# Attention maxima split and transposed by quad, with PSUM handed out by single banks

## The chip, the cores and the metric

One core of one Trainium2 chip runs the whole kernel. The metric is the device time of one execution in microseconds; it is quoted as the median of several runs. Five engines work from queues of their own, each strictly in the order in which it was written: TensorE (PE; its weight loads are shown as PEld), VectorE (DVE), ScalarE (ACT), GpSimd (POOL) and SyncE (SP), which here issues nearly all DMAs.

## The reference

A decoder block on x of 8 batches x 256 tokens x 128 features, in float32, with a context of 64 tokens for each batch:

```python
x = layernorm(x + self_attn(x))                # 16 heads of 8 dims, rotary q and k, no mask
x = layernorm(x + cross_attn(x, ctx, mask))    # 16 heads, 64 keys, mask * -1e9, a dense layer behind it
x = layernorm(x + relu(x @ W1 + b1) @ W2 + b2) # 128 -> 512 -> 128

scores = einsum('bhqd,bhkd->bhqk', q, k) / sqrt(8)
probs = softmax(scores, axis=-1)               # needs the maximum over the keys of each query and head
ctx = einsum('bhqk,bhkd->bhqd', probs, v)
```

## The kernel before

The 16 heads of the self-attention are four *quads* g of four heads each. For each batch b, quad g and half t of the queries, `max_scores(b, g, t)` (L603) writes the scores with queries on the partitions (use `Mgt`, 128 x 1024) to PSUM, and VectorE's `reduce(b, g, t)` (L1535) takes the maximum over the keys of four heads. When all eight reductions of a batch are done, `split_max(b)` (L1541, L1545) turns the maxima of all quads into a high and a low part in two instructions. `max_transposes(b)` (L613) transposes them on TensorE (use `mT`), and ScalarE's `maxT(b)` (L1193) copies them, 32 rows by 1024 columns, below the query rows of `q_rows`. Only then come the second scores: `exp_scores(b, g, half)` (L625, uses `Egh`, 128 x 1024) has keys on the partitions and subtracts the maxima in the same product, because `k_diag` has rows that pick the head (`diag_heads`, `head_of_row`). `exp(b, g, half)` (L1202) on ScalarE makes the probabilities, and `pv(b, half)` (L642) multiplies them with v.

The cross-attention has the same form with fewer keys: `maxx_scores` (`Xm`, L699), `reduce(b, "x", t)` (L1532), `split_maxx`, `maxx_transposes` (`mxT`), `maxxT` (L1234), `expx_scores` (`Y`, L718), `expx` (L1246) and `pvx` (L731). Its mask is put into PSUM ahead of each product by `preset_mask`: 22 times on ScalarE (L1163) and 10 times on VectorE (L1665). Behind it are a dense layer (L759), the feed-forward layers `ffn_up` (L779) and `ffn_down` (L790), and three layer norms. ScalarE's other copies out of PSUM are `pv_copy` (L1209) and `pvx_copy` (L1256).

The q and k of a batch go through DRAM to be laid out: GpSimd rotates them (`rope_cosine`, `rope_sine`, `rope_sum`, `qk_high`, `qk_low`), SP writes images to `z_self` and reads them back with `load_q(b)` (L369, one DMA) and `load_k(b)` (L377, four DMAs). There are two copies of `q_rows` and `k_diag`, so both loads of batch b wait, in `rows_free`, until all eight `E` products of batch b - 2 are made. The first two batches are rotated on VectorE instead (`first_products`, `first_rotated`, `first_low`).

PSUM is five *spaces*: `s0`, `s1` and `s2` of two banks each, `b0` and `b1` of one bank. A table `USES` lists for each space all its uses in order, written out by a search; `TURN` gives the place of a use, and each engine waits for the reader of the use before (`earlier`). A small use in `s0` to `s2` holds both banks. The order of all calls on each of the five engines is a list written out by hand or by a search as well: hundreds of calls on TensorE, VectorE and ScalarE, about a hundred on GpSimd and on SP.

## Time and profile before

| what | us |
|---|---|
| median of 3 runs | 221.43 (220.69 to 223.17) |
| the profiled execution, its own time | 223.62 |
| its span, from the first to the last instruction | 221.8 |
| busy: PE, PEld, DVE, ACT, POOL | 202.8, 152.1, 173.4, 166.1, 93.6 |
| mean granted TensorE clock | 0.988 of full speed |

The profile is of one execution. Matmul ends are modelled and matmuls are pipelined, so that "PE busy" counts some time in which a product only drains. Lines of a timeline merge instructions of one group: start, time from the first start to the last end, engine, line, what it writes and reads, how many, and in brackets the idle time of the engine before it with what ended it.

### The profile page before, as it was taken

Reading aid. Unit: us, or ns where it says so; the run is one execution under the profiler, and the core shown is the slowest. Engines: PE = TensorE matmul, PEld = TensorE weight load, DVE = VectorE, ACT = ScalarE, POOL = GpSimd, SP = SyncE. Lnnn points to the kernel's source line nnn. Section 1 sums busy time; section 2 is a strip of 40 time slices with the busy share of each in tenths; the row PEclk is TensorE's granted clock in tenths of the full one; section 3 lists DMA queues with packets and bytes.
Section 4 is the critical chain, followed back from the end, with each engine's and each line's share of the span. In section 5 each row is a group of like instructions: output and inputs, shape, how many; then the busy total and the mean of one; then the engine's idle time right before and its main releaser. Section 6 shows DMA issues by size and latency. Waiting matters only on the chain.

```text
span 221.8 us, 5032 instructions
## 1 busy us (share of the span) xinstructions
PE 202.8 (91%) x1632; PEld 152.1 (69%) x1632; DVE 173.4 (78%) x346; ACT 166.1 (75%) x248; POOL 93.6 (42%) x130
## 2 busy tenths in 40 slices
PE   7777989999898979999989998999999999999991
PEld 5555657666476546767657667776987868977991
DVE  6585998448967987848988977898788879885764
ACT  2256567778188678969998898999899997896360
POOL 9304997048085776903103600710261343221533
PEclk9996999999999999999999999999999999999998
DMA  6967639414558861743650361140230234100011
GB/s 195 400 194 219 188 86 334 115 54 159 164 173 269 206 184 36 236 145 103 192 176 5 113 192 55 56 143 1 75 92 0 99 98 112 65 3 24 23 53 47
DMA packets 21354, 28.20 MB, mean 127 GB/s; under 512 B 5424, under 2 KB 16688, under 8 KB 21328
## 3 DMA queue, kind: packets, MB, share of 16 engines
q1 hardware_dynamic: 20696, 27.08, 39.8%
q10 hardware_dynamic: 632, 0.79, 1.3%
q8 instruction: 14, 0.23, 0.4%
q14 instruction: 12, 0.10, 0.2%
HBM read 14.76 MB, written 11.27 MB: 117 GB/s over the span
## 4 chain that ended last, share of the span: by engine, by line
PE 66%; issue 6%; DVE 6%; ACT 5%; DMA 2%; SPq 1%; POOLq 0%; POOL 0%; ACTq 0%; DVEq 0%
PE bank L642 12%; PE scores L625 11%; PE scores L603 10%; ACT probs L1202 4%; PE bank L779 4%; PE scores L699 3%; PE bank L790 3%; PE scores L718 3%; PE scores L779 3%; PE bank L731 3%; PE scores L790 2%; DVE max_parts L1535 2%; DMA k_diag<-z_self 2%; PE bank L671 1%; PE bank L759 1%
## 5 line engine op out<-in xcount | busy, mean ns | idle before, releaser
L1535 DVE TENSOR_REDUCE max_parts<-scores 128x4 f32<-128x1024 f32 x64 | 75.7, 1217 | 18.3 <-PE scores L603 18.1
L1202 ACT ACTIVATE probs<-scores 128x1024 f32<-128x1024 f32 x64 | 63.3, 1025 | 8.0 <-PE scores L625 7.4
L603 PE MATMUL scores<-k_diag,q_rows 96*128 96x512 f32 x128 | 44.0, 434 | 6.4 <-issue 4.2
L625 PE MATMUL scores<-q_rows,k_diag 128*128 128x256 f32 x256 | 43.0, 297 | 2.3 <-ACT probs L1202 1.3
L625 PEld LDWEIGHTS scores<-q_rows,k_diag 128*128 128x128 f32 x256 | 34.5, 189 | 12.3 <-issue 7.4
L603 PEld LDWEIGHTS scores<-k_diag,q_rows 96*128 96x128 f32 x128 | 20.7, 193 | 15.5 <-issue 13.7
L1973 POOL TENSOR_TENSOR rstd<-mean_var,minus_half 128x2 f32<-128x2 f32 x23 | 15.8, 696 | 36.1 <-DVE mean_var L1569 36.0
L642 PE MATMUL bank<-probs,v_ones 128*32 128x256 f32 x512 | 30.9, 382 | 0.1
L1163 ACT COPY scores<-cross_sb 128x1024 f32<-128x1024 f32 x22 | 22.4, 1028 | 2.5 <-DVE maxx_parts L1532 2.0
L642 PEld LDWEIGHTS bank<-probs,v_ones 128*32 128x32 f32 x512 | 15.6, 109 | 11.7 <-issue 3.3
L1532 DVE TENSOR_REDUCE maxx_parts<-scores 128x16 f32<-128x1024 f32 x16 | 19.1, 1216 | 3.9 <-PE scores L699 3.9
L1980 POOL TENSOR_TENSOR sum<-att,xT_sb 128x256 f32<-128x256 f32 x8 | 5.9, 738 | 28.5 <-DVE att L1615 28.4
L1999 POOL TENSOR_TENSOR qx_parts<-qx_parts 128x256 fp32r<-128x256 f32 x8 | 5.8, 728 | 27.2 <-ACT qx_parts L1226 27.2
L1246 ACT ACTIVATE probsx<-scores 128x1024 f32<-128x1024 f32 x16 | 16.2, 1028 | 0.8 <-PE scores L718 0.7
L2025 POOL TENSOR_TENSOR qk_sin<-qk_swapped,rope_sb 128x256 f32<-128x256 f32 x12 | 8.5, 728 | 18.2 <-DMA qk_swapped<-qk 18.2
L1576 DVE TENSOR_SCALAR x<-sum,mean_var,rstd 128x128 f32<-128x128 f32 x32 | 11.8, 409 | 2.5 <-POOL rstd L1973 2.5
L1665 DVE COPY scores<-cross_sb 128x1024 f32<-128x1024 f32 x10 | 12.2, 1218 | 0.7 <-ACT probsx L1246 0.5
L718 PE MATMUL scores<-qx_slots,kx_diag 128*128 128x256 f32 x64 | 11.0, 296 | 0.7 <-ACT qx_slots L1234 0.7
L699 PE MATMUL scores<-kx_diag,qx_slots 96*128 96x256 f32 x64 | 11.2, 300 | 0.4 <-issue 0.4
L1209 ACT COPY ctxvT<-bank 128x256 f32<-128x256 f32 x16 | 5.8, 372 | 7.0 <-PE bank L642 7.0
L718 PEld LDWEIGHTS scores<-qx_slots,kx_diag 128*128 128x128 f32 x64 | 8.8, 189 | 2.5 <-ACT qx_slots L1234 1.3
L1565 DVE BATCH_NORM_STATS2 stats<-sum 128x6 f32<-128x128 f32 x42 | 10.0, 279 | 0.2
(174 smaller groups left out, 358.4 us busy)
## 6 DMA issues: line engine op xcount, KB each, us to landing
z_self<-qk_parts SPq DMA_DIRECT2D x21, 256.0 KB, 2.7
q_rows<-z_self SPq DMA_DIRECT2D x8, 384.0 KB, 4.1
qx_slots<-z_qx SPq DMA_DIRECT2D x8, 384.0 KB, 3.6
k_diag<-z_self SPq DMA_DIRECT2D x30, 96.0 KB
z_qx<-qx_parts SPq DMA_DIRECT2D x8, 256.0 KB, 2.2
qk_swapped<-qk SPq DMA_DIRECT2D x12, 128.0 KB, 2.8
xT_sb<-x SPq DMA_DIRECT2D x4, 256.0 KB, 3.3
z_qx<-qx_parts SPq DMA_DIRECT2D x8, 128.0 KB, 1.7
```

Of the source, the lines that this page charges most:

```text
L603: mm = pe.matmul(score(use, b)[:, h * S:(h + 2) * S], qr_r[0:NROWS, b % 2, g, t * P:(t + 1) * P], kd_r[0:NROWS, b % 2, h:h + 2, g, :], sta ...
L625: mm = pe.matmul(score(use, b)[:, (2 * j + kt) * S:(2 * j + kt + 1) * S], kd_r[:, b % 2, 2 * half + j, g, kt * P:(kt + 1) * P], qr_r[:, b ...
L642: mm = pe.matmul(misc(use, b)[STRIP * h:STRIP * (h + 1), 0:S], v_ones[:, b % 2, kt, HQ * g + h, cell], probs[:, g, h, kt, :], start=(g % 2 ...
L699: mm = pe.matmul(score(use, b)[:, g * 256:(g + 1) * 256], qxs_r[0:NROWS, b % 2, g, t * P:(t + 1) * P], kxd_r[0:NROWS, b % 2, g, :, :], sta ...
L718: mm = pe.matmul(score(use, b)[:, (p % 4) * S:(p % 4 + 1) * S], kxd_r[:, b % 2, p // 2, 2 * (p % 2):2 * (p % 2) + 2, :], qxs_r[:, b % 2, p ...
L779: mm = pe.matmul(misc(use, b)[:, j * S:(j + 1) * S], const("w1")[:, c * P:(c + 1) * P], x2T_of[turn(b)], start=True, stop=True)
L1163: ins = nc.scalar.copy(score(use, b).rearrange("p (n c) -> p n c", c=SC if use[0] == "X" else S), mask)
L1202: ins = nc.scalar.activation(probs[:, g, 2 * half:2 * half + 2, :, :], score(use, b), ACT.Exp, scale=KSCALE)
L1246: ins = nc.scalar.activation(probsx[:, 4 * half:4 * half + 4, :], score(use, b), ACT.Exp)
L1532: ins = nc.vector.tensor_reduce(quads(maxx_parts, b, 1)[:, t * QUADS:(t + 1) * QUADS, 0:HQ], score(use, b).rearrange("p (g h k) -> p g h k ...
L1535: ins = nc.vector.tensor_reduce(max_parts[:, b % 2, 1, t, g * MROWS:g * MROWS + HQ], score(use, b).rearrange("p (h k) -> p h k", h=HQ), AX ...
L1973: nc.gpsimd.tensor_tensor(rstd[:, k, :], mean_var[:, k, :, 1], minus_half[:], ALU.pow).then_inc(rstd_done[n], 1)
```

## The change

- Each quad is split alone: `split_max(b, g)` takes 8 maxima of each partition (4 heads by 2 halves), `max_transposes(b, g)` transposes both halves in one step (a 128 x 64 block, the halves 32 rows apart), and `maxT(b, g)` copies 8 rows by 128 columns twice. `exp_scores(b, g, half)` waits for its own quad's copy alone. There are 32 such steps in place of 8.
- The cross-attention's maxima stay in one step for each batch, but their block is 32 wide for each quad, and `maxxT` copies 8 rows by 256 columns four times in place of 32 rows by 1024 once.
- The other rows of `q_rows` and `qx_slots` must be zero: GpSimd clears both at the start (`clear_rows`, `clear_qx`), and `load_q`, `load_qx`, `maxT` and `maxxT` wait for that. VectorE clears `max_parts` and `maxx_parts` in `clear_parts`, which now stands ahead of its `clear_diag`.
- PSUM is eight single banks. Scores take a pair (0-1, 2-3, 4-5 or 6-7) and small uses one bank; `earlier` is now a list of waits, one for each different use before.
- All orders and the table of banks are new. Presets of the mask are 17 on ScalarE and 15 on VectorE. On VectorE `kx_split` and `place_vx(0)` come behind batch 0's reductions, on SP `load_cross` and `load_ctxT` behind batch 0's q and k.

```diff
 USES = {
-    "s0":
-        "qp.0 v.4 kp.1 vxa.0 M01.0 M21.0 M31.0 M00.1 M30.1 E10.0 E21.0 E11.0 E31.0 mT.1 E00.1 M01.2 M31.2 E20.1 "
...
+    0:
+        "qkp.5 M20.0 M01.0 M10.0 mT0.0 E31.0 M20.1 E20.0 E10.0 E01.1 E00.1 M20.2 E31.1 E10.2 mT0.2 M20.3 M21.3 "
...
+    1:
+        "M20.0 M01.0 M10.0 mT1.0 E31.0 M20.1 E20.0 E10.0 PV0.0 E01.1 E00.1 M20.2 E31.1 E10.2 M20.3 M21.3 E20.2 "
...
-        scores = psum("scores", [P, 3, 1024])
-        bank = psum("bank", [P, 2, 512])
+        banks = psum("banks", [P, BANKS * BANK])
...
         def earlier(use, b):
 
-            space, before = TURN[use, b]
-            return read[space], before
+            return [taken(*previous) for previous in dict.fromkeys(TURN[use, b][2])]
...
-            def max_transposes(b):
-                pe.wait_ge(max_split, b + 1)
+            def max_transposes(b, g):
+                pe.wait_ge(max_split[g], b + 1)
                 pe.wait_ge(wv_in, 16)
-                if TURN["mT", b][1]:
-                    pe.wait_ge(*earlier("mT", b))
-                for t in range(QT):
-                    mm = pe.transpose(misc("mT", b)[0:XROWS, t * P:(t + 1) * P], max_parts[:, b % 2, 0, t, :], ident)
-                written_by(mm, "mT", b)
+                for previous in earlier(f"mT{g}", b):
+                    pe.wait_ge(*previous)
+                mm = pe.transpose(misc(f"mT{g}", b)[0:QT * STRIP, 0:P], max_parts[:, b % 2, g, :, :], ident)
+                written_by(mm, f"mT{g}", b)
 
             def exp_scores(b, g, half):
                 use = f"E{g}{half}"
-                pe.wait_ge(*taken("mT", b))
+                pe.wait_ge(*taken(f"mT{g}", b))
...
-            def maxT(b):
-                act.wait_ge(*made("mT", b))
+            def maxT(b, g):
+                act.wait_ge(*made(f"mT{g}", b))
+                act.wait_ge(rows_zeroed, 1)
                 if b > 1:
-                    for products in all_made(EXPONENTS, b - 2):
-                        act.wait_ge(*products)
-                ins = nc.scalar.copy(q_rows[max_rows, b % 2, :, :].bitcast(F32R),
-                                     misc("mT", b)[0:XROWS, 0:S].rearrange("p (o c) -> p o c", o=1).to_broadcast([XROWS, QUADS, S]))
-                read_by(ins, "mT", b)
+                    act.wait_ge(*made(f"E{g}0", b - 2))
+                    act.wait_ge(*made(f"E{g}1", b - 2))
+                for t in range(QT):
+                    ins = nc.scalar.copy(q_rows[max_rows, b % 2, g, t * P:(t + 1) * P].bitcast(F32R),
+                                         misc(f"mT{g}", b)[t * STRIP:t * STRIP + MROWS, 0:P])
+                read_by(ins, f"mT{g}", b)
...
-            def split_max(b):
-                for maxima in all_taken(MAXIMA, b):
-                    dve.wait_ge(*maxima)
-                if b > 1:
-                    dve.wait_ge(*made("mT", b - 2))
-                split(max_parts, b, max_hi_done, max_split)
+            def split_max(b, g):
+                dve.wait_ge(*taken(f"M{g}0", b))
+                dve.wait_ge(*taken(f"M{g}1", b))
+                exact = max_parts[:, b % 2, g, :, MROWS:MROWS + HQ].rearrange("p t (h o) -> p t h o", o=1)
+                nc.vector.tensor_reduce(max_parts[:, b % 2, g, :, 0:HQ].bitcast(F32R), exact, AX.X, ALU.max, negate=True
+                                        ).then_inc(max_hi_done[g], 1)
+                dve.wait_ge(max_hi_done[g], b + 1)
+                both = max_parts[:, b % 2, g, :, 0:2 * MROWS].rearrange("p t (a h) -> p t h a", a=2)[:, :, 0:HQ, :]
+                nc.vector.tensor_reduce(max_parts[:, b % 2, g, :, HQ:MROWS], both, AX.X, ALU.add, negate=True
+                                        ).then_inc(max_split[g], 1)
...
             clear_y()
+            clear_parts()
             clear_diag()
             first_products(0, 1)
             first_rotated(0, 1)
+            first_low(0, 1)
             first_products(0, 0)
-            first_low(0, 1)
```

## Rows read from the trace of the kernel before

**Rows 1.** The page, part 1: busy time, share, instructions of each engine

```profile
PE 202.8 (91%) x1632; PEld 152.1 (69%) x1632; DVE 173.4 (78%) x346; ACT 166.1 (75%) x248; POOL 93.6 (42%) x130
```

**Rows 2.** Windows of three stages: length, busy us of each engine (instructions), granted clock

```profile
32.00:80.00 48.00, 43.81 (x376) 29.83 (x374) 35.37 (x52) 33.01 (x42) 27.45 (x41) 1.00 0.61 178
80.00:137.00 57.00, 53.98 (x468) 38.35 (x469) 46.91 (x77) 51.75 (x68) 19.86 (x29) 1.00 0.44 134
137.00:214.00 77.00, 76.18 (x662) 62.35 (x661) 63.42 (x165) 65.55 (x109) 25.09 (x36) 1.00 0.19 58
```

**Rows 3.** Timeline of VectorE and ScalarE between batches, 41 to 63 us

```profile
46.72 0.36 DVE L1613 RECIPROCAL recip<-bank 128x32 f32<-128x32 f32 x1 [5.00 <-PE bank L654]
...
57.27 0.37 ACT L1209 COPY ctxvT<-bank 128x256 f32<-128x256 f32 x1 [1.59 <-PE bank L642]
60.28 0.37 ACT L1209 COPY ctxvT<-bank 128x256 f32<-128x256 f32 x1 [2.63 <-PE bank L642]
...
62.42 1.00 ACT L1193 CAST q_rows<-bank 32x1024 fp32r<-32x1024 f32 x1
```

**Rows 4.** Timeline of SP's loads of batches 2 and 3, and TensorE's first maxima products

```profile
41.64 3.03 SPq L377 DMA_DIRECT2D k_diag<-z_self  x4
...
54.57 2.98 SPq L377 DMA_DIRECT2D k_diag<-z_self  x4
...
47.37 1.22 PE L603 MATMUL scores<-k_diag,q_rows 96*128 96x512 f32 x4 [0.21 <-issue]
...
61.07 0.70 PE L603 MATMUL scores<-k_diag,q_rows 96*128 96x512 f32 x2 [0.86 <-issue]
```

**Rows 5.** Timeline of the start, from the first products to the first exponential

```profile
5.87 0.48 DVE L1587 SCALAR_TENSOR_TENSOR qk_cos<-scores,wk_sb,rope_sb 128x256 f32<-128x256 f32 x1 [0.47 <-DMA rope_sb<-rope]
...
19.17 2.36 DVE L1535 TENSOR_REDUCE max_parts<-scores 128x4 f32<-128x1024 f32 x2 [1.90 <-PE scores L603]
...
19.70 1.40 POOL L2025 TENSOR_TENSOR qk_sin<-qk_swapped,rope_sb 128x256 f32<-128x256 f32 x2 [11.95 <-DMA qk_swapped<-qk]
...
22.28 6.88 DVE L1535 TENSOR_REDUCE max_parts<-scores 128x4 f32<-128x1024 f32 x6 [0.76 <-PE scores L603]
...
29.25 0.19 DVE L1541 TENSOR_REDUCE max_parts<-max_parts 128x32 fp32r<-128x32 f32 x1
...
30.27 1.00 ACT L1193 CAST q_rows<-scores 32x1024 fp32r<-32x1024 f32 x1 [0.78 <-PE scores L613]
...
32.19 1.02 ACT L1202 ACTIVATE probs<-scores 128x1024 f32<-128x1024 f32 x1
```

**Rows 6.** Groups by line and form: shapes, count, busy us, mean ns of one

```profile
L1541 DVE TENSOR_REDUCE max_parts<-max_parts 128x32 fp32r<-128x32 f32 x8 | 1.5, 186 | 0.6 <-DVE max_parts L1535 0.2
L1545 DVE TENSOR_REDUCE max_parts<-max_parts 128x32 f32<-128x64 f32 x8 | 1.8, 221 | 0.3
L1193 ACT CAST q_rows<-scores 32x1024 fp32r<-32x1024 f32 x5 | 5.0, 1000 | 2.2 <-PE scores L613 2.2
L1209 ACT COPY ctxvT<-bank 128x256 f32<-128x256 f32 x16 | 5.8, 372 | 7.0 <-PE bank L642 7.0
L1256 ACT COPY attvT<-bank 128x512 f32<-128x512 f32 x7 | 4.1, 589 | 0.3 <-PE bank L731 0.2
L1163 ACT COPY scores<-cross_sb 128x1024 f32<-128x1024 f32 x22 | 22.4, 1028 | 2.5 <-DVE maxx_parts L1532 2.0
L1665 DVE COPY scores<-cross_sb 128x1024 f32<-128x1024 f32 x10 | 12.2, 1218 | 0.7 <-ACT probsx L1246 0.5
L1631 DVE TENSOR_SCALAR attvT<-bank,cross_sb 128x512 f32<-128x512 f32 x1 | 0.8, 750 | 0.0
```

**Rows 7.** The chain that ended last: start, us, what

```profile
30.01 0.22 PE scores L613 x2
...
67.35 0.70 PE scores L603 x2
...
145.46 0.47 PE scores L603 x2
```

More of the change, by code:

```diff
@@ L120, in turns @@
     at = {}
-    for space, uses in USES.items():
-        for before, use in enumerate(uses.split()):
+    for bank in range(BANKS):
+        signals, previous = 0, None
+        for use in USES[bank].split():
             name, b = use.split(".")
-            at[name, int(b)] = space, before
+            key = name, int(b)
+            if key not in at:
+                at[key] = bank, signals, []
+                signals += 1
+            if previous:
+                at[key][2].append(previous)
+            previous = key
     return at
@@ L561, in warm_up @@
                 for _ in range(3):
-                    pe.matmul(bank[:, 1, 0:S], y[:, 0, :], y[:].rearrange("p t d -> p (t d)"), start=True, stop=True)
+                    pe.matmul(banks[:, 7 * BANK:7 * BANK + S], y[:, 0, :], y[:].rearrange("p t d -> p (t d)"), start=True, stop=True)
             def first_proj(b, j):
@@ L1156, in preset_mask @@
                 act.wait_ge(mask_ready, 1)
-                act.wait_ge(*earlier(use, b))
+                for previous in earlier(use, b):
+                    act.wait_ge(*previous)
                 if use[0] == "X":
@@ new lines, in _ @@
+            expx(3, 1)
+            exp(7, 3, 0)
+            exp(7, 2, 1)
+            maxxT(4)
+            exp(7, 2, 0)
+            expx(4, 1)
+            pv_copy(7, 0)
+            x2T_copy(1)
+            pvx_copy(3)
+            pv_copy(7, 1)
+            expx(4, 0)
+            x1T_copy(6)
+            preset_mask("Xm1", 5)
+            qx_copy(6)
+            att2T_copy(3)
+            preset_mask("Y1", 5)
+            relu(1, 0)
+            pvx_copy(4)
+            maxxT(5)
+            relu(1, 1)
@@ L1773, in _ @@
+            reduce(0, 1, 1)
+            split_max(0, 3)
+            reduce(0, 1, 0)
+            split_max(0, 0)
+            split_max(0, 1)
+            split_max(0, 2)
+            kx_split()
+            place_vx(1)
+            reduce(1, 0, 1)
+            reduce(1, 1, 0)
+            reduce(1, 2, 0)
+            place_vx(0)
+            reduce(1, 1, 1)
+            reduce(1, 2, 1)
+            split_max(1, 2)
+            scale_mask()
+            split_max(1, 1)
             reduce(1, 0, 0)
+            split_max(1, 0)
@@ L1854, in _ @@
[L1854 to L1868 removed]
+            split_max(6, 0)
+            reduce(6, 3, 1)
+            reduce(6, 2, 0)
```

1445 lines of the change are left out of this document (737 added, 708 removed), and 58 rows, old and new, of the table USES.

## The prediction, made before the changed kernel was run

> **What bounds the kernel now.** I read the page's busy shares first. TensorE is the fullest engine at 202.8 us of a span of 221.8, with VectorE at 78% and ScalarE at 75% [rows 1]. A mean over the span hides three different stages, so I then cut the span into windows. From 32 to 80 us no engine is full: VectorE is busy 35.4 of 48 us, ScalarE 33.0, and TensorE's weight loads, which stand for how many products went through, fill 29.8 us, or 62% [rows 2]. From 80 to 137 us ScalarE is busy 51.8 of 57 us (91%), VectorE 82%, weight loads 67%. From 137 to 214 us weight loads fill 81% and matmuls 76.2 of 77 us: there TensorE is the bound, because the feed-forward layers need almost nothing of the others.
>
> What takes the time of the first stage is seen between the batches. After the split of batch 1's maxima VectorE sits idle for 5.00 us. ScalarE sits idle for 1.59 and then 2.63 us after the last exponential of batch 1, and gets batch 2's maxima only at 62.42 us [rows 3]. A batch is a chain of phases: eight reductions, one split, one transpose, one copy, eight exponentials. One of the two readers of PSUM is often without work while the other has its phase. The second link is the load of q and k: it waits for all E products of two batches earlier, SP issues k's DMAs from 41.64 to 44.67 us, and the first maxima product of batch 2 starts at 47.37; for batch 3 they start at 54.57 and the product comes at 61.07 [rows 4]. So a load costs some 6 us from k's first DMA, and what releases it is the end of the phase of exponentials.
>
> The chain that ended last shows the third loss: a pair of maxima products takes 0.47 us when the PSUM space is free and 0.70 us when TensorE must stop for it or behind it [rows 7].
>
> **The start.** The first exponential starts at 32.19 us, behind eight reductions of batch 0 (19.17 to 29.16), a split at 29.25, and a copy of 1.00 us from 30.27 [rows 5]. After the change the first split follows the seventh reduction, which saves one reduction of 1.15 us (6.88 us for six). The copy is two of 128 columns. ScalarE took 372 ns for 256 columns and 589 ns for 512 [rows 6], 0.85 ns a column, so 128 columns are 0.26 us each and the copy 0.53 in place of 1.00. Only one weight block is transposed in place of two: 0.11 us less. The smaller split saves under 0.1. Sum: 1.15 + 0.47 + 0.11 + 0.1 = 1.8 us, and I take -1.8. Against it stand VectorE's two new clearings of 512 elements, at most half a preset copy of 1.22 us each and so 1.2 us, of which 0.47 is hidden by the wait for the rotary table [rows 5], and `first_low(0, 1)`, which now stands with its wait for ScalarE ahead of q's products. For it, `load_cross` and `load_ctxT` no longer compete with the first loads, and k's DMAs, the last to be issued before, go ahead of q. I take these at nothing between them, with bounds of -1 and +1.5 us. GpSimd's two further clearings lie in the 11.95 us for which it is idle ahead of 19.70 us [rows 5]; without the cover `load_q(0)` waits, and the whole start with it.
>
> **What is added.** VectorE: a split of 32 elements takes 186 ns and one of 64 elements 221 ns [rows 6], so 1.1 ns an element over a fixed 151. With 8 and 16 elements it is 160 + 169 = 0.33 us for a quad, 10.5 us for 32 quads, less the 3.3 of before: +7.2 us. Five presets of the mask come over at 1.22 us: +6.1. `kx_split` and `place_vx(0)` (0.75 us for the first instruction [rows 6], some 2 us in all as an estimate from it) move out of an idle time into the run of reductions: +2. The sum is about +15 us, of which 0.9 (four quads less the old split of 0.41) falls to batch 0. ScalarE: 64 copies at 0.263 us less eight at 1.00 are +8.8. `maxxT` with 32 copies at 0.372 in place of eight at 1.00 is +3.9. Five presets at 1.03 leave: -5.1. The sum is +7.6 us. TensorE: 32 transposes in place of 16 at 0.11 (0.22 for two [rows 7]) are +1.8 us, and each is a point at which it can stop: between 0 and 32 times the 0.23 us by which 0.70 exceeds 0.47, so 0 to 7.4 us. I take 1.6 for the last stage's share of all this. The further waits on the lists of banks have no row of their own; between nothing and 0.05 us for each score product (an estimate, a tenth of a 0.47 us pair), I take nothing, since the engines' queues run ahead of satisfied waits.
>
> The Trainium skill ("VectorE: DVE Perf Modes", section on the TRN2 errata) speaks against this change: a fixed latency is paid for each instruction, and tiles should have 512 elements or more. The trace agrees as to size, since its fixed part of 151 ns [rows 6] is near the page's some 150 cycles; by the rule alone the change is a loss of the whole sum above.
>
> **What is gained.** In 32 to 214 us VectorE is busy 145.7 of 182 us and ScalarE 150.3 [rows 2]. After the change VectorE has about 160 us to do there and ScalarE about 158. With the start 1.8 us earlier, an unchanged time needs VectorE's idle time to fall from 36 to 24 us. Can it? Between batches the 5.00 us and the 4.2 us of rows 3 go for the most part: the exponentials of the first quad run beside the reductions of the last. The last E product of a batch then comes 2 to 3 us earlier against its first reduction, and the load of the batch after next with it. A fourth pair of banks also lets a product be ready while both readers are at work. For 32 to 80 us, where all engines are under 75% but for modelled matmul time, I take -2.8 us, net of the added work: more than one bubble of 5 us is removed, and 3.5 us of splits and copies are added. For 80 to 137 us ScalarE at 91% and VectorE at 82% take up what the finer steps free: 0, with bounds of -2 and +4. For 137 to 214 us TensorE is full: +1.6.
>
> The Trainium skill ("Perfetto Trace Analysis", Identifying the Most-Contended Engine) holds that matmul busy time misleads, and that the share of weight loads tells the headroom. By its rule the last stage at 81% would have up to a fifth to give, some 14 us as an estimate. The 0.47 us pair in that stage [rows 7] is without a stop, so the trace does not show such a headroom.
>
> The sum: -1.8 - 2.8 + 0 + 1.6 = -3.0 us. The profiled execution took 223.62 us, 1.8 more than its span, and stands 2.2 above the median of 221.43; I take the difference from the median: 218.4.
>
> **The rivals.**
>
> *A fuller flow.* The barrier costs at every junction, not only at the first two, and the fourth pair of banks removes most 0.70 us stops. Then 80 to 137 us gives 2 to 3 us as well and the first stage 4 or 5: 214.5. For it speaks that the loop from E products through a load to the maxima products is shortened for each batch. Against it, VectorE would have to be over 92% busy for 180 us.
>
> *VectorE becomes the bound (slower).* Its added 15 us lie in the stages in which it feeds everything: splits sit in its queue ahead of reductions, and each reduction holds two banks. It decides from the point at which less than 12 us of its idle time is recovered. If just the bubble of 5.0 us and some 3 us more go, the time is +15 - 8 - 1.8 = +5 us: 226.5. For it: no stage of the kernel before has all three engines at nearly 90%. Against it: the idle time is mostly waiting for TensorE, which the additions do not load. The skill's rule on small tiles, above, would lead here.
>
> *A draw.* The idle time is only exchanged for small instructions, and the earlier start is given back before the last stage: 221.4.
>
> *It does not do what it says.* If the order lists let each quad's transposes wait in TensorE's queue behind products of other batches, exponentials start no earlier within a batch. That has the price of the second rival, and I count it there.
>
> **How the numbers follow.** Chances: forecast 0.42, fuller flow 0.13, draw 0.22, VectorE the bound 0.23. About 1% (2.2 us) is what a measurement of this kernel can tell from no change. Four fifths of the forecast's share lie under 219.2 us, as does all of the fuller flow; so faster 0.47. The draw and the rest of the forecast, and a small part of the third case, make same 0.29; slower 0.24. The bounds of the start (-1, +1.5), of the middle stage (-2, +4) and of TensorE's stops reach from 213 to 225, which leaves a tenth out on either side.
>
> **What would show it.** The first exponential at about 30.4 us in place of 32.19. VectorE busy near 188 us and ScalarE near 174. No idle time of over 3 us on VectorE between 35 and 65 us. The last exponential of the self-attention 4 to 5 us earlier, and a last stage that is 1 to 2 us longer. The prediction is wrong if the first maxima product comes after 19 us, if VectorE's idle time ends mostly on TensorE still, or if ScalarE's small copies take much over 0.26 us.

## The result

The changed kernel takes 225.77 us (224.91 to 226.56, 4 executions), the kernel before beside it 221.06 us (220.33 to 223.17, 4 executions): a ratio of 1.019, 95% interval 1.015 to 1.023. It is slower by 4.2 us by the ratio and 4.7 by the medians. The forecast was 218.4 us and a gain. Its profiled execution took 225.86 us, 1.86 more than its span of 224.0 us. Executions over 1.5% above the fastest of their kernel are left out of every ratio in this text.

Busy shares first, as in [rows 1]:

```profile
PE 205.4 (92%) x1648; PEld 155.3 (69%) x1648; DVE 185.9 (83%) x401; ACT 173.5 (77%) x323; POOL 97.7 (44%) x132
```

Then the three stages, as in [rows 2], the last one up to the end of the span, and below them that last stage of the kernel before, also up to its end:

```profile
32.00:80.00 48.00, 45.73 (x394) 32.26 (x393) 42.24 (x80) 37.52 (x65) 30.78 (x44) 1.00 0.60 185
80.00:137.00 57.00, 54.43 (x470) 38.46 (x468) 49.56 (x92) 51.62 (x91) 18.75 (x27) 1.00 0.43 128
137.00:224.00 87.00, 79.80 (x688) 64.89 (x686) 72.02 (x193) 69.00 (x135) 27.17 (x39) 0.99 0.19 57
...
137.00:221.80 84.80, 79.30 (x688) 65.28 (x686) 67.04 (x180) 65.97 (x109) 27.02 (x39) 0.99 0.19 59
```

VectorE has 12.5 us more to do and ScalarE 7.4. VectorE's idle time fell from 48.4 us (221.8 - 173.4) to 38.1, so 10.3 us were recovered where the prediction put the break-even at 12. In the first stage more products were done than before (394 against 376), so the flow there is fuller, as intended. It is given back later: from 137 us to its end the kernel before takes 84.8 us (221.8 - 137) and the changed one 87.0, with 688 products in both. The two profiled executions are 2.2 us apart in span, since that of the kernel before stands above its median; so the stages show about half of the loss of 4.7 us.

The costs of the small instructions, by form:

```profile
L1227 ACT CAST q_rows<-banks 8x128 fp32r<-8x128 f32 x64 | 16.3, 255 | 6.6 <-PE banks L620 5.6
...
L1270 ACT CAST qx_slots<-banks 8x256 fp32r<-8x256 f32 x32 | 11.6, 363 | 0.9 <-PE banks L715 0.3
...
L1600 DVE TENSOR_REDUCE max_parts<-max_parts 128x8 f32<-128x16 f32 x32 | 5.5, 171 | 1.1
...
L1596 DVE TENSOR_REDUCE max_parts<-max_parts 128x8 fp32r<-128x8 f32 x32 | 4.9, 152 | 0.6
```

These are the estimates of the prediction (0.263, 0.372, 0.169 and 0.160 us) within 6%. The sizes of the added work were right; what they do to the time was not.

The start, beside [rows 5]:

```profile
8.64 0.48 DVE L1640 SCALAR_TENSOR_TENSOR qk_cos<-banks,wq_sb,rope_sb 128x256 f32<-128x256 f32 x1
...
18.99 2.07 PE L611 MATMUL banks<-k_diag,q_rows 96*128 96x512 f32 x4 [3.84 <-DMA q_rows<-z_self]
...
23.70 5.75 DVE L1588 TENSOR_REDUCE max_parts<-banks 128x4 f32<-128x1024 f32 x5 [1.10 <-PE banks L611]
...
29.37 0.15 DVE L1596 TENSOR_REDUCE max_parts<-max_parts 128x8 fp32r<-128x8 f32 x1
...
29.90 1.31 ACT L1202 CAST kx_diag<-wv_sb 8x256 fp32r<-8x256 f32 x4
31.11 2.15 ACT L1227 CAST q_rows<-banks 8x128 fp32r<-8x128 f32 x8
...
33.82 1.04 ACT L1236 ACTIVATE probs<-banks 128x1024 f32<-128x1024 f32 x1
```

The first exponential comes at 33.82 us, not at 30.4, and 1.6 us after that of before (32.19). The first maxima product is 0.86 us late (18.99 against 18.13). These two distances belong to this execution: in another one of the same kernel (`after_again`, below) the first maxima product comes at 18.19 and the first exponential at 31.31. After seven reductions the first split stands at 29.37, later than the split after eight was before (29.25). A transposed quad must then wait for ScalarE, which is at `kx_heads` until 31.21, and all eight copies are made in one run, so the quads are not taken one by one.

From the wait ahead of those first scores up to 24 us TensorE ran at the lower of its two clock levels (1.2 GHz in place of 2.4). Windows of 2 us; the last but two column is the granted clock:

```profile
16.00:18.00 2.00, 0.00 (x0) 0.00 (x0) 0.92 (x2) 0.73 (x2) 2.00 (x2) 0.79 0.88 230
18.00:20.00 2.00, 1.01 (x2) 0.83 (x3) 0.00 (x0) 0.00 (x0) 1.76 (x1) 0.50 1.04 310
...
22.00:24.00 2.00, 1.96 (x7) 1.27 (x7) 0.90 (x2) 1.50 (x4) 1.80 (x4) 0.51 0.99 381
```

The fall comes in the 3.84 us in which TensorE waits for the q rows. The profiled execution of the kernel before has such a fall too, a shorter one, behind a wait of 2.29 us:

```profile
18.00:20.00 2.00, 1.87 (x5) 1.50 (x6) 0.83 (x1) 1.93 (x4) 0.29 (x1) 0.59 0.93 300
20.00:22.00 2.00, 2.00 (x6) 1.58 (x6) 1.52 (x2) 0.27 (x1) 2.00 (x3) 0.56 0.38 96
```

The chain that ended last also has two pieces that [rows 7] did not have: SP's four loads of kx for batch 2 (line 427, 113.44 to 116.96 us) and batch 3 (131.87 to 135.1), ahead of the load of qx:

```profile
131.87 3.22 SPq L427 DMA_DIRECT2D kx_diag<-z_kx  x4
...
135.26 0.38 SPq L445 DMA_DIRECT2D qx_slots<-z_qx  x1
```

So five explanations stood side by side: (A) the small instructions themselves, (B) the order, with the cross-attention late, (C) the late start, (D) the kx loads, and, from the spread of the executions, (G) TensorE's clock. A sixth question (E) was what single banks are worth without the quads, and a seventh (F, H) whether quads pay in an order that fits them.

### The profile page after: what moved, and what is told of

It is laid out like the page before. It is cut to its first block, busy times and chain, and to the rows that moved or that the text cites. A ratio compares the mean times of both kernels' runs of the same rounds, so it can differ in the third digit from the quotient of the medians.

```text
span 224.0 us, 5412 instructions
## 1 busy us (share of the span) xinstructions
PE 205.4 (92%) x1648; PEld 155.3 (69%) x1648; DVE 185.9 (83%) x401; ACT 173.5 (77%) x323; POOL 97.7 (44%) x132
## 4 chain that ended last, share of the span: by engine, by line
PE 63%; DVE 13%; issue 8%; DMA 5%; ACT 5%; SPq 4%; POOL 1%; POOLq 0%; DVEq 0%; ACTq 0%
PE banks L649 13%; PE banks L632 10%; PE banks L611 9%; DVE max_parts L1588 7%; PE banks L797 6%; PE banks L786 5%; PE banks L725 4%; SPq L427 3%; PE banks L706 3%; PE banks L738 3%; DMA q_rows<-z_self 3%; PE banks L766 2%; DMA qx_slots<-z_qx 2%; PE banks L748 2%; PE banks L620 1%
## 5 line engine op out<-in xcount | busy, mean ns | idle before, releaser
L1588 DVE TENSOR_REDUCE max_parts<-banks 128x4 f32<-128x1024 f32 x64 | 75.9, 1218 | 15.3 <-PE banks L611 15.3
L1236 ACT ACTIVATE probs<-banks 128x1024 f32<-128x1024 f32 x64 | 63.4, 1025 | 4.0 <-PE banks L632 2.9
L611 PE MATMUL banks<-k_diag,q_rows 96*128 96x512 f32 x128 | 44.2, 434 | 5.7 <-DMA q_rows<-z_self 3.8
L632 PE MATMUL banks<-q_rows,k_diag 128*128 128x256 f32 x256 | 42.9, 296 | 1.6 <-DVE vx_ones L1697 0.5
L632 PEld LDWEIGHTS banks<-q_rows,k_diag 128*128 128x128 f32 x256 | 34.7, 189 | 11.2 <-issue 8.4
L649 PE MATMUL banks<-probs,v_ones 128*32 128x256 f32 x512 | 30.9, 382 | 0.8 <-DVE max_parts L1588 0.3
L611 PEld LDWEIGHTS banks<-k_diag,q_rows 96*128 96x128 f32 x128 | 20.7, 197 | 12.1 <-issue 6.5
L1588 DVE TENSOR_REDUCE maxx_parts<-banks 128x16 f32<-128x1024 f32 x16 | 19.3, 1216 | 2.6 <-PE banks L706 2.5
L1719 DVE COPY banks<-cross_sb 128x1024 f32<-128x1024 f32 x15 | 18.1, 1219 | 1.0 <-ACT probs L1236 0.6
L1195 ACT COPY banks<-cross_sb 128x1024 f32<-128x1024 f32 x17 | 17.5, 1032 | 0.6
```

The costliest lines, as they stand in the source:

```text
L611: mm = pe.matmul(score(use, b)[:, h * S:(h + 2) * S], qr_r[0:NROWS, b % 2, g, t * P:(t + 1) * P], kd_r[0:NROWS, b % 2, h:h + 2, g, :], sta ...
L632: mm = pe.matmul(score(use, b)[:, (2 * j + kt) * S:(2 * j + kt + 1) * S], kd_r[:, b % 2, 2 * half + j, g, kt * P:(kt + 1) * P], qr_r[:, b ...
L649: mm = pe.matmul(misc(use, b)[STRIP * h:STRIP * (h + 1), 0:S], v_ones[:, b % 2, kt, HQ * g + h, cell], probs[:, g, h, kt, :], start=(g % 2 ...
L1195: ins = nc.scalar.copy(score(use, b).rearrange("p (n c) -> p n c", c=SC if use[0] == "X" else S), mask)
L1236: ins = nc.scalar.activation(probs[:, g, 2 * half:2 * half + 2, :, :], score(use, b), ACT.Exp, scale=KSCALE)
L1588: ins = nc.vector.tensor_reduce(out, score(use, b).rearrange("p (h k) -> p h k", k=SC if g == "x" else S), AX.X, ALU.max)
```

## The experiments

All ratios are to the kernel before in the same job, whose median there was 222 to 223 us. All re-ordered kernels below move whole calls on an engine's list, change the table of banks, and may give a mask preset to the other of its two engines; no other instruction is altered by it.

**The small instructions at the old places.** `quads_coarse` is the kernel before, with

```
 def split_max(b):
-    split(...)                      # all quads at once, 2 instructions
+    for g in range(QUADS):
+        split_quad(b, g)            # 8 instructions
 def maxT(b):
-    nc.scalar.copy(q_rows[max_rows, ...], misc("mT", b)[...])
+    for g in range(QUADS):
+        for t in range(QT):
+            ins = nc.scalar.copy(q_rows[max_rows, b % 2, g, t * P:(t + 1) * P].bitcast(F32R), ...)
```

and the changed kernel's four copies for `maxxT` and its clearings. The order of the calls and the uses of PSUM are those of the kernel before.

> The kernel before with its own order on all engines and its own PSUM spaces; only the maxima are split quad by quad (8 small splits instead of 2), transposed by 4 instructions of 64 rows instead of 2 of 128, and copied by 8 copies of 8 rows instead of one of 32 rows, all at the places of the old ones, and the exponents still wait for all of them. It carries the added small work of the change and none of what that work buys. Added in each batch between the last reduction and the first exponent: 6 splits more (about 1.0 us), 2 transposes more (0.4 us), and 7 copies of 0.25 us (1.8 us) less what the one large copy took (1.0 us): some 2 us, 8 times. Theory A (the small instructions cost the time): this stretch is a barrier in every batch, so 230 to 238 us. Theory B (order: the added work is hidden behind other engines' work and the loss of the changed kernel comes from its order): 221 to 225 us here.

It took 235.03 us: ratio 1.055 (1.048 to 1.062). The chain that ended last shows the barrier; its columns are start, length, what:

```profile
30.72 0.25 ACT q_rows L1220
...
32.57 0.26 ACT q_rows L1220
32.84 0.14 issue
32.97 0.73 PE banks L648 x4
```

`q_rows` copies have 6% of that chain. From the end of a batch's last reduction to the end of its last copy the eight batches together take 46.1 us here and 31.0 in the kernel before, 1.9 us more for each. So the small instructions, those of the cross-attention with them, cost 12 us when they stand on the barrier. The changed kernel is slower by 4 us alone; but it has the single banks and another order as well, so this run does not say how much of the 12 us it hides behind other work.

**Half of the small instructions out of the changed kernel.** `after_light` leaves out the second split instruction and the copy for the last 128 queries, so the low part of the maxima is zero, and for half of the queries the rows of `q_rows` stay as `clear_rows` left them: no maximum is subtracted there.

> The changed kernel with half of the added small work of the self-attention left out: each quad's split keeps its first instruction and leaves out the second, so that the low part of the maxima stays zero (32 VectorE instructions of 171 ns, 5.5 us), and each quad's maxima are copied to the rows of q for the first 128 queries alone (32 ScalarE copies of 255 ns, 8.2 us). TensorE's work and all orders stay. Theory A (the small instructions cost the time): 13.6 us of work on the two engines less, half of it on the path between maxima and exponents, so the time falls by 4 to 7 us, to 219 to 222 us. Theory B (order): both engines idle 17 and 23 per cent of the span, and the last 40 us are bound by TensorE's own order, so it falls by at most 2 us, to 224 us or more.

224.9 us, ratio 1.008 (1.004 to 1.013), against 1.019 for the changed kernel: about 1.1%, 2.4 us, for 13.6 us of work. That is below what A asked for, and B's limit of 2 us lies within the noise of this difference (some 0.6%, from the two intervals). The small instructions have a part that is clear of noise; whether the order has one is not decided here.

**The start repaired.** `after_start`:

```
-            clear_parts()
             clear_diag()
             first_products(0, 1)
             first_rotated(0, 1)
-            first_low(0, 1)
             first_products(0, 0)
+            first_low(0, 1)
             first_rotated(0, 0)
             first_low(0, 0)
+            clear_parts()
```

> The changed kernel; on VectorE the clearing of the maxima tiles (0.96 us) goes from ahead of the first products to behind them, and the low part of q's first image goes back behind the second pair of products. Everything else is as in the changed kernel. Theory C (the late start, first exponent at 33.8 instead of 32.2 us, reaches the end): the first scores come about 1.1 us earlier and the time falls by 1 to 1.6 us, to 224.3 to 224.8 us. Theories A and B (the start is absorbed, since the self-attention of batches 3 to 6 runs 4 to 7 us ahead anyway): within 0.5 us of the changed kernel, 225.3 to 226 us.

Ratio 1.016 (1.010 to 1.023). The ratio is 0.3% less than 1.019, well inside the interval. Its first exponential is at 32.88 us, 0.94 earlier than in the changed kernel's execution above, but the edit can't be given that: `after_loads`, the next run, has the unchanged start and its first exponential at 32.77. So C is not decided by this run: the start's order is worth some 0.6 us at most by the ratios, and nothing that the trace shows.

**The kx loads behind qx.** `after_loads`:

```
-            load_kx(2)
             qx_image_high(2)
             ...
             load_qx(2)
+            load_kx(2)
```

and the same for batch 3.

> The changed kernel; on SyncE the loads of kx for batches 2 and 3 (four DMAs each) stand behind the load of qx of the same batch instead of ahead of it. Theory D (these loads stand on the path: the chain has SyncE at 113.4 to 117.0 and 131.9 to 135.1 us, with qx's load behind them): each of the two stretches gives back about 3 us to the cross-attention of batches 2 and 3, and if that is what ends last, the time falls by 1.5 to 3 us, to 223 to 224.5 us. Theories A and B: the cross-attention of these batches waits for TensorE's order anyway, so within 0.6 us of the changed kernel.

Ratio 1.016 (1.010 to 1.023). The trace shows the load of qx for batch 3 freed, and its product not. SP's queue, then TensorE:

```profile
130.91 0.32 SPq L445 DMA_DIRECT2D qx_slots<-z_qx  x1
...
137.72 0.72 PE L706 MATMUL banks<-kx_diag,qx_slots 96*128 96x256 f32 x4 [0.22 <-ACT banks L1195]
```

The load is issued at 130.91 in place of 135.26 us, 4.35 earlier; the maxima product of that batch starts at 137.72 in place of 138.90, and the whole of these 1.18 us was already there at 114 us (another product of the line starts at 113.69 in place of 114.93). It stood on TensorE's list behind other work. D falls, by the trace and not by the ratio: a piece of the chain that ended last is not a piece that costs.

**The changed kernel again**, as a standard:

> The changed kernel itself once more, as the standard for the runs beside it: 1.015 to 1.023 times the kernel before.

Ratio 1.0185 (1.008 to 1.029). Its executions gave G: (clock, us) were (1.000, 224.24), (0.988, 227.28), (0.976, 228.02) and (0.965, 230.15), while the seven of before beside it had 0.996 to 1.000. A line through the four has 1.6 us for each 0.01 of the mean clock. That is a hint and no more: it rests on the two longest, which are not in the ratio, and in the four executions of the result above the fastest (224.91 us) has 0.984 and the slowest (226.56) 0.991.

The profiled execution of this run, at 224.24 us, is the same kernel as that of the result, at 225.86, and has no fall of the clock. It shows what the start is without one:

```profile
16.00:18.00 2.00, 0.00 (x0) 0.00 (x0) 1.48 (x2) 0.92 (x3) 2.00 (x3) 1.00 1.00 278
18.00:20.00 2.00, 1.81 (x12) 1.65 (x12) 1.05 (x1) 0.14 (x1) 2.00 (x1) 1.00 1.06 251
...
18.19 1.19 PE L611 MATMUL banks<-k_diag,q_rows 96*128 96x512 f32 x4 [2.32 <-DMA q_rows<-z_self]
...
31.31 1.04 ACT L1236 ACTIVATE probs<-banks 128x1024 f32<-128x1024 f32 x1
```

TensorE waited 2.32 us instead of 3.84, the q rows having landed earlier, and kept its clock; the first exponential comes 2.51 us earlier than at 33.82, and the span is 1.9 us shorter (222.1 against 224.0). How much of this is the clock and how much the earlier landing, two executions do not tell.

**Re-ordered from the first call on.** Three kernels, the order of before and of the changed kernel searched by moving one call at a time with durations from the profiles.

> The kernel before with its own instructions (one split and one 32-row copy of the maxima per batch) and its own five PSUM spaces; only the order of the calls on every engine, the space of each use and the engine of the mask presets are searched anew: one call moved at a time, kept when the end comes earlier with the durations read from the profile. Theory B (what the order is, is worth several us either way, and the changed kernel has an order that delays the cross-attention): a better order exists for the old instructions too: 212 to 218 us on the scale where before is 221.4. Theory A (only the work counts; the old order was as good as its work allows): 219.5 to 222.5 us.

> As the re-ordered kernel before, from the same starting order and with the same search, but PSUM is kept by eight single banks, so that a transposed tile or a projection takes one bank where it took a space of two; the maxima are still split, transposed and copied batch by batch. If single banks are worth something by themselves (theory E), it is 2 to 5 us faster than the re-ordered kernel before: 209 to 215 us on the scale where before is 221.4. If they are worth nothing, within 1 us of it.

> The changed kernel with its quad-wise maxima and its single banks, its start repaired as in the run of the start, and orders, banks and places of the presets searched anew in the same way and with the same effort. Theory B: the changed kernel's loss lay in its order, so this is well below it, 213 to 218 us, and below the kernel before. Theory A, in the form that the added small work costs the same in any order: it stays 3 to 6 us above the kernel with single banks and batch-wise maxima that was searched with the same effort. Theory F (quad-wise maxima pay once the order fits them): it is as fast as that kernel or faster.

Ratios 1.070 (1.062 to 1.078), 1.070 (1.062 to 1.078) and 1.092 (1.085 to 1.098): all far slower than either kernel. They say nothing of A, B or E, since two things went wrong. The first is likely the larger, because one execution of `before_order` kept a mean clock of 0.999 and still took 235.64 us. They had been costed with a score product group at 0.48 us and no delay between a signal and TensorE's next product; measured when nothing kept it waiting the group takes 0.55, and the delay is 0.145. Second, TensorE lost its clock in the start. Windows of `before_banks_order`:

```profile
20.00:30.00 10.00, 7.38 (x24) 4.94 (x24) 9.03 (x8) 5.82 (x13) 9.68 (x12) 0.83 0.66 201
30.00:40.00 10.00, 8.64 (x26) 6.15 (x27) 8.58 (x10) 4.82 (x6) 6.59 (x11) 0.53 0.58 162
```

In these three kernels some mask presets of the cross-attention were placed behind a narrow tile in their banks (3, 11 and 11 of the 32), and the three kernels give wrong results; that the masks of those score tiles are lost is the likely reason, see the last section.

**Re-ordered from 45 us on**, with the start as it is and each preset behind a full score tile:

> The kernel before with its own instructions and its five PSUM spaces; the order of the first 45 us is left as it is on every engine, and the rest is re-ordered by moving one call at a time with the durations read from the profiles so far; each mask preset stays behind a full score tile in its space. The three kernels that were re-ordered from the first call on lost TensorE's clock (mean grant 0.95 to 0.97, with stretches near 0.5 between 20 and 50 us), which this leaves out. Theory B (order is worth several us): 216 to 219 us on the scale where before is 221.4. Theory A (before's order is as good as its work and its five spaces allow): 220 to 223 us.

> The same search and the same frozen start of the kernel before, with PSUM kept by eight single banks; the maxima stay batch by batch. Theory E (single banks by themselves are worth something, because a projection or a transposed tile no longer blocks two banks): 2 to 5 us faster than the one with five spaces, 213 to 217 us. If they are worth nothing, within 1 us of it.

> The changed kernel, quad-wise maxima and single banks, with its start repaired and frozen up to 45 us, and the rest re-ordered by the same search with the same effort. Theory B (the changed kernel's loss is its order): 213 to 218 us, below both kernels. Theory A (the small instructions cost the time in any order): 3 us or more above the re-ordered kernel with single banks and batch-wise maxima, 217 to 222 us. Theory F (quad-wise maxima pay for themselves once the order fits): within 1 us of that kernel or below it, although its start is 1 us later.

Ratios 1.022 (1.016 to 1.029), 1.010 (1.004 to 1.015) and 1.020 (1.011 to 1.028). Every theory's number was missed: none is faster than before. Only the order among the three is of use, since single banks helped by 1.2%. The durations were still the wrong ones.

**TensorE kept at work in the start's wait.** `after_busy` and `before_busy`:

```
+            def keep_busy(n):
+                for previous in earlier("M30", 0):
+                    pe.wait_ge(*previous)
+                for _ in range(n):
+                    pe.matmul(misc("M30", 0)[:, 0:S], y[:, 0, :], y[:].rearrange("p t d -> p (t d)"), start=True, stop=True)
...
             qk_proj(7)
+            keep_busy(8)
             max_scores(0, 3, 0)
```

> The changed kernel with 8 products of the zeroed y tile (256 columns each, written to the bank of the first score tile ahead of it, read by nobody) between the last early projection and the first score product of batch 0, where TensorE waited 3.84 us for the q rows. Nothing else changes. Theory G (part of the loss is TensorE's clock: in the executions so far the mean grant was 0.983 for the changed kernel and 0.992 to 0.998 for the one before, the fall comes right behind this wait, and over the executions of one kernel 0.01 of clock went with 1.6 us of time): the clock goes to 0.995 or more and the time falls by 1 to 2.5 us, to a ratio of 1.008 to 1.014. If the clock has no part, the ratio stays at 1.018.

> The kernel before with 5 such products in the same place, where TensorE waited 2.29 us. Theory G: its clock was already 0.992 to 0.998 in the mean, so it gains 0 to 1 us, and its executions scatter less. If the clock has no part: no change, or up to 0.4 us slower where a product is still running when the rows land.

`after_busy` has 1.011 (1.006 to 1.015) against 1.0185 and 1.019 without; `before_busy` 1.002 (0.999 to 1.006). In the trace of `after_busy`:

```profile
18.00:20.00 2.00, 2.00 (x14) 1.77 (x13) 1.00 (x1) 0.10 (x1) 1.66 (x1) 1.00 1.02 280
...
22.00:24.00 2.00, 2.00 (x13) 1.67 (x12) 2.00 (x3) 2.00 (x4) 1.87 (x3) 1.00 0.86 338
```

The clock stays at 1.00 through the wait, VectorE is at work in all of 20 to 24 us, the reductions run without a stop, and the first exponential is at 31.35 us, 2.47 earlier. So the products keep the clock up in the start, and the fall is part of what made it late. What that is worth at the end stays open. By the ratios it is 0.8%, some 1.8 us, but the two kernels were measured beside different executions of the kernel before, and the interval of `after_busy` only touches that of the result (1.015) and lies inside that of `after_again` (1.008 to 1.029). `after_again`'s execution at clock 1.00 without the products took 224.24 us, and the one profiled here 225.39, with the first exponential at the same time to 0.04 us. In two of the six executions the mean clock was still 0.98 and 0.99. For the kernel before the products are worth nothing that can be measured; its first exponential in `before_busy` is at 31.18:

```profile
31.18 1.02 ACT L1208 ACTIVATE probs<-scores 128x1024 f32<-128x1024 f32 x1
```

**The measured costs in the search.** The same re-ordering, now with 0.55 us for a group of score products and the 0.145 us, and with `keep_busy` in the start:

> Single banks with batch-wise maxima, the same 5 products, the first 45 us in before's order, and the rest re-ordered once more, now with the cost that each call had in the traces when nothing kept it waiting (a group of score products 0.55 us, not 0.48) and 0.145 us from a signal to TensorE's next product. Theory E (single banks are worth 2 to 4 us once the order uses them): 215 to 219 us on the scale where before is 221.4. If the earlier re-ordered kernels failed because before's order can't be bettered: 221 us or more.

> The changed kernel's own calls (quad-wise maxima, single banks, its own first 45 us with 8 such products), the rest re-ordered in the same way and with the same effort as the run beside it. Theory B (the loss is the order of the changed kernel): 217 to 221 us on the scale where before is 221.4, so well below the changed kernel. Theory A (the small instructions cost the time in any order): 3 us or more above the kernel beside it. Theory F (quad-wise maxima pay once the order fits): as fast as that kernel, although its first scores come 1 us later.

> The kernel before with its own five PSUM spaces and batch-wise maxima, 5 products in the wait of the start, its first 45 us as they are, and the rest re-ordered with the measured costs as in the run with single banks that came to 217.1 us (ratio 0.972). Theory E (the single banks carry that gain): 2 to 5 us slower than that run, 219 to 222 us. If the order alone carries it: within 1 us of it, 216 to 218 us.

> Quad-wise maxima on single banks again, but started from the order of the 217.1 us run and with before's first 25 us on every engine (GpSimd's two clearings ahead of it), and re-ordered from there with the same effort. It tells whether the 6.6 us between batch-wise and quad-wise maxima come from the changed kernel's own start and order, which the run of 223.7 us still had in its first 45 us. If they do (theory H): 217 to 219 us. If the small instructions cost the time in any order (theory A: VectorE 10 us more than the batch-wise kernel, ScalarE 8 us more, 16 more points at which TensorE can stop): 3 us or more above the batch-wise run, 220 to 224 us.

> The run of 217.1 us (batch-wise maxima, single banks, 5 products in the start's wait), re-ordered a little further, now from 25 us on. If what limits it is still the order: 1 to 2 us faster, 214.5 to 216.5 us on the scale where before is 221.4. If TensorE's own work, busy 202 of 214.5 us, leaves no more: within 1 us of 217.1.

| kernel | maxima | PSUM | ratio to before | 95% interval |
|---|---|---|---|---|
| before_busy (before's order) | batch | five spaces | 1.002 | 0.999 to 1.006 |
| before_order3 | batch | five spaces | 0.990 | 0.985 to 0.995 |
| before_banks3 | batch | single banks | 0.972 | 0.968 to 0.975 |
| before_banks4 | batch | single banks | 0.973 | 0.968 to 0.977 |
| after_order3 (changed kernel's start) | quad | single banks | 1.002 | 0.998 to 1.007 |
| quads_order (before's start) | quad | single banks | 1.000 | 0.997 to 1.003 |
| after_busy (changed kernel's order) | quad | single banks | 1.011 | 1.006 to 1.015 |

The lines are read in pairs that differ in one feature of the kernel; each line has an order of its own from the same search, so how well the search did is part of every distance. A new order alone takes 1.2% off the kernel before. Single banks take a further 1.7 to 1.8%, so E holds. Quads in place of batches put 2.7 to 3.1% on, whichever start they have: A holds, F and H fall. The changed kernel's own order is 0.8% worse than what the same search found for the same calls. That is in the direction of B, but at 221.9 us on the scale where before is 221.4 it misses B's forecast of 217 to 221, and the two intervals just touch; B holds in a small part at most. The part of B that blamed the late cross-attention falls: its first exponentials start at 79.10 us in `quads_order` and at 91.21 in `after_order3`, and the two take the same time.

Summed up, `keep_busy` +0.2, a searched order -1.2, single banks -1.8, quads +3.1 and the changed kernel's order +0.8 give the 1.1% of `after_busy`. These are the steps between the lines of the table, so the sum is no check of them. The last 0.8%, from 1.011 to the 1.019 of the changed kernel, is what the start's clock may be worth. `before_banks4`, with more freedom, is no faster than `before_banks3`: the search found nothing more, with TensorE busy 94%.

Where the quads lose it is seen in the pages of `before_banks4` (span 214.9 us) and `quads_order` (220.9):

```profile
PE 201.3 (94%) x1642; PEld 153.6 (71%) x1642; DVE 177.8 (83%) x349; ACT 163.9 (76%) x245; POOL 93.7 (44%) x130
...
PE 75%; ACT 8%; issue 6%; DVE 4%; DMA 4%; SPq 1%; POOLq 0%; POOL 0%; ACTq 0%; DVEq 0%
```

```profile
PE 204.8 (93%) x1658; PEld 156.2 (71%) x1658; DVE 181.4 (82%) x399; ACT 175.5 (79%) x325; POOL 97.1 (44%) x132
...
PE 64%; DVE 9%; issue 9%; ACT 8%; DMA 5%; SPq 3%; POOLq 0%; POOL 0%; ACTq 0%; DVEq 0%
```

Of the 6.0 us, 3.5 are more busy time of TensorE and 2.5 more idle time (16.1 against 13.6). The transposes are part of the first, 32 in place of 16, busy 7.8 us against 3.1 in the groups below, some of it overlapping other products. The second is, by the chain, TensorE made to wait on the two readers: VectorE's share of the chain goes from 4 to 9%, and the groups by line give the reductions' own wait on TensorE as 11.5 against 8.2 us, so both sides stop more often:

```profile
L1560 DVE TENSOR_REDUCE max_parts<-banks 128x4 f32<-128x1024 f32 x64 | 75.0, 1216 | 8.2 <-PE banks L629 8.0
...
L639 PE MATMUL banks<-wv_sb,max_parts 128*32 128x128 f32 x16 | 3.1, 275 | 0.8 <-DVE max_parts L1570 0.7
```

```profile
L1597 DVE TENSOR_REDUCE max_parts<-banks 128x4 f32<-128x1024 f32 x64 | 75.7, 1218 | 11.5 <-PE banks L617 11.1
...
L626 PE MATMUL banks<-wv_sb,max_parts 128*64 128x128 f32 x32 | 7.8, 275 | 0.3
```

## Why the prediction was wrong

The sizes of the added instructions, each engine's added work (VectorE +12.5 us against +15, ScalarE +7.4 against +7.6) and the place where the flow would be fuller were right. These steps of the sum were not.

*The start, -1.8 us, measured +1.6 in the profiled pair and +0.1 with the clock at 1.00 in both.* The second figure is the first exponential of `after_again` (31.31) against that of `before_busy` (31.18). So the gain was not there even in an undisturbed start. The prediction added up what each step of the new phase takes and left out who stands on the engines at that moment. `kx_heads` on ScalarE (1.31 us at 29.90, at 27.39 in `after_again`) took the place in which the first quad should have been copied, and the eight copies were then made in one run. The rest of the +1.6, some 1.5 us, belongs to the execution: there the first scores came 0.86 us late and TensorE made them at half clock for longer than in the kernel before, so that the seventh reduction ended no earlier than the eighth had. The list under "What would show it" named the first product after 19 us as a sign; it came at 18.99. The clock was no term at all, although the rows of the kernel before have its fall, 0.59 and 0.56 from 18 to 22 us. By the ratios it is worth some 0.8% of the changed kernel's time, and that size was not settled.

*The first stage, -2.8 us.* The idle times of [rows 3] did go: between 35 and 66 us VectorE has none over 1.53 us. More products were done in that stage, as forecast. But the sum treated this as time won at the end. What the stage gained, 18 products, was self-attention run ahead of need: the last self-attention exponential ends at 169.6 us, against 168.9 before and not 4 to 5 us earlier as the prediction asked for, and the first exponentials of batch 0's cross-attention start at 92.95 in place of 81.40 us. The work that the end waits for had not come earlier. That the late cross-attention itself cost time is not shown (`quads_order`, with it at 79.10, is no faster than `after_order3`). By a better order the search could win back 0.8%.

*The middle stage, 0, and the last, +1.6.* From 137 us to the end it is +2.2 us. The bound of 0 to 7.4 us for TensorE's extra stops held the truth, 1.6 was too little: `quads_order` shows 3.5 us of busy time and 2.5 us of waiting, 6.0 in all.

*What was gained by the banks.* The prediction gave single banks no term of their own, only the fourth pair as a part of the fuller flow. They are the one part of the change that is shown to pay, 1.7 to 1.8%, and the rival of the fuller flow had this mechanism. But they pay 4 us, and the quads cost 6.

The rival that came true is the second, VectorE becoming the bound: 226.5 us by its own sum, 225.77 measured, with its condition (less than 12 us of idle time recovered) met at 10.3. In `after_again`'s execution VectorE is idle for 36.0 us (222.1 - 186.1) and 12.4 are recovered, so the condition is met only at its edge. That its number fits so well is in part luck: it holds the start's -1.8 us, which did not come, and 15 us of added work where 12.5 were measured. Its mechanism is only half right. VectorE is not full in any stage (88% at most), and what it costs is paid in TensorE's stops and extra products. It had a chance of 0.23, too low, because the gain side of the sum was taken from idle time of engines that do not bound. The rule weighed there, a fixed latency for each instruction on the page "VectorE: DVE Perf Modes" of the Trainium skill (TRN2 errata), points the right way; the whole sum of the added work as a loss, which it would give, is too much, since `quads_coarse` lost 12 us with the same instructions on a barrier and `quads_order` 6. The headroom by weight loads that the Trainium skill gives ("Perfetto Trace Analysis", Identifying the Most-Contended Engine) is not settled by these runs. From 137 us to the end `before_banks3` took 77.5 us where before took 84.8, with the share of weight loads at 78% (60.5 us) against 77% (65.3 us):

```profile
137.00:214.50 77.50, 72.82 (x636) 60.50 (x635) 63.45 (x168) 60.63 (x101) 24.53 (x35) 1.00 0.19 58
```

But only 636 products were left for that stage instead of 688, and each took 0.122 us of it as against 0.123. The stage ended sooner because more had been done ahead of it (502 products from 80 to 137 us, 468 before), and no run made the stage itself faster.

## What to carry over

Splitting a step to let its successor start sooner pays only if the successor's engine is free then and if the work brought forward is what the end waits for. So look in the trace at who stands on each queue in that moment, and follow the last stage back, before taking idle time as a gain. Changes that come together should be told apart at equal effort in the order: here the bank bookkeeping was worth 4 us and was hidden behind a split that cost 6. And the first exponential moved by 2.5 us between two executions of one kernel, so a difference in the start that rests on one trace of each kernel is worth a second trace. A version with single banks, batch-wise maxima, and a few idle products in the start's wait is faster than both kernels: `before_banks3`, 0.972 (0.968 to 0.975) of the kernel before.

## What the runs showed of the hardware

- TensorE's clock can fall to half in or behind the wait ahead of the first scores, and stays there for some 3 to 7 us. In the ten profiled executions that have the first calls of either kernel and nothing in the wait it fell behind waits of 1.77 (`before_order2`), 2.29, 3.20, 3.49, 3.51 and 3.84 us, and did not behind 1.84, 1.90, 2.32 and 2.74; the changed kernel is in both lists (3.84 and 2.32). With products of zeros in the wait it stayed at 1.00 in the start in all seven profiled executions. What a fall costs at the end is not settled: 0.01 of the mean clock went with 1.6 us in the four executions of `after_again` and with nothing clear in those of the result.
- Between the end of the instruction that signals and the start of the one that waited lie, as medians over all the traces, 0.145 us for a TensorE product behind VectorE or ScalarE, 0.037 us for ScalarE and VectorE behind TensorE, and for GpSimd 0.08 us behind VectorE and 0.14 behind ScalarE. The re-orderings that were costed with the first of these and with 0.55 us for a score group came out 2 to 4% faster than those that were not; they had the products in the wait as well.
- A preset of PSUM that score products are to be added to seems to hold only where the use of the bank before it wrote the bank in full. The three kernels with presets behind narrow tiles give wrong results; all others have none so placed. No run varied this alone, so it is argued and not shown.
